# Attention in an encoder block: from 96-row bf16 stacks to paired 64-row fp32r stacks

## What is computed

```python
qkv = layernorm(x) @ qkv_w.T + qkv_b          # 16 heads of 16 channels
q, k = rotary(q), rotary(k)
attn = softmax(einsum('bhqd,bhkd->bhqk', q, k) * D ** -0.5)
x = x + einsum('bhqk,bhkd->bhqd', attn, v).reshape(B, L, C) @ proj_w.T + proj_b
x = x + cross_attention(layernorm(x), ctx)
x = x + experts(layernorm(x))                 # each expert takes its top 512 tokens
```

## Time and profile before

| | |
|---|---|
| median of 3 runs | 1540.33 us (1540.18 to 1541.49) |
| profiled execution | 1540.64 us, span 1538.8 us |
| busy in the span: PE, DVE, ACT, POOL | 84%, 74%, 50%, 23% |
| mean granted TensorE clock | 0.886 of full |

### The profile page before, as it was taken

The page is one execution under the profiler, slowest core; times in us unless marked ns, Lnnn a source line. Parts: engine busy times, 40 slices in busy tenths (PEclk is TensorE's granted clock), DMA queues, the critical chain, the costliest instruction groups (busy, mean ns, idle before and its releaser), DMA issues. The chain is left out here.

```text
span 1538.8 us, 21970 instructions
## 1 busy us (share of the span) xinstructions
PE 1297.3 (84%) x7046; PEld 618.8 (40%) x7046; DVE 1132.2 (74%) x2543; ACT 770.7 (50%) x984; POOL 354.2 (23%) x327
## 2 busy tenths in 40 slices
PE   5777488999999999999999999976788613799995
PEld 3444212222222222222222222235677602678794
DVE  6888487889888898789888898325777487677751
ACT  2333203666666666566666666833434311365652
POOL 3777530000000000000000000011332102266654
PEclk9888656999999999999999999986778655899998
DMA  3246492023330333113331200041232101163532
GB/s 118 93 150 192 155 192 56 20 48 62 60 60 12 59 63 60 30 40 62 60 63 21 47 7 5 9 140 45 95 99 82 55 4 55 43 156 99 158 86 28
DMA packets 100871, 111.19 MB, mean 72 GB/s; under 512 B 24992, under 2 KB 77984, under 8 KB 99744
## 3 DMA queue, kind: packets, MB, share of 16 engines
q1 hardware_dynamic: 94624, 101.50, 25.7%
q0 software_dynamic: 6144, 8.39, 2.9%
HBM read 71.73 MB, written 37.75 MB: 71 GB/s over the span
## 5 line engine op out<-in xcount | busy, mean ns | idle before, releaser
L623 DVE TENSOR_REDUCE b_max_halves<-banks 128x1 f32<-128x512 f32 x1024 | 635.8, 683 | 82.4 <-PE banks L678 70.1
L591 ACT ACTIVATE b_probs<-banks 128x1024 f32<-128x1024 f32 x512 | 496.5, 1021 | 313.9 <-PE banks L736 312.7
L678 PE MATMUL banks<-b_k,b_q 96*128 96x512 bf16 x1024 | 354.7, 401 | 30.8 <-DVE b_identb L644 17.3
L736 PE MATMUL banks<-b_q,b_k 99*128 99x512 bf16 x1024 | 302.1, 382 | 1.7 <-DMA b_q<-b_max_rows 0.2
L703 PE MATMUL banks<-b_probs,b_v 128*32 128x512 f32 x2048 | 274.5, 608 | 0.5 <-ACT b_probs L591 0.5
L678 PEld LDWEIGHTS banks<-b_k,b_q 96*128 96x128 bf16 x1024 | 85.0, 97 | 410.0 <-DVE b_max_halves L623 351.0
L607 POOL TENSOR_SCALAR b_minus_max<-b_max 128x32 f32<-128x32 f32 x16 | 4.6, 290 | 741.4 <-DVE b_max L627 741.4
L736 PEld LDWEIGHTS banks<-b_q,b_k 99*128 99x128 bf16 x1024 | 94.2, 98 | 109.0 <-ACT b_probs L591 55.6
L1373 POOL DMA_INDIRECT e_x<-rows,d_idx x32 | 52.3, 1635 | 127.0 <-DVE d_wx L1554 64.1
L359 PE MATMUL banks<-a_w,a_xnT 128*128 128x512 f32 x128 | 73.4, 703 | 1.2 <-issue 1.2
L1682 PE MATMUL banks<-e_w2h,e_hTh 128*128 128x256 f32 x256 | 73.8, 288 | 0.0
(11 more groups left out here) (228 smaller groups left out, 1710.1 us busy)
## 6 DMA issues: line engine op xcount, KB each, us to landing
e_w<-in_w SPq DMA_DIRECT2D x16, 1024.0 KB, 8.3
v_tiles<-a_v SPq DMA_DIRECT2D x8, 1024.0 KB, 6.0
b_v<-v_tiles SPq DMA_DIRECT2D x16, 512.0 KB, 9.7
q_stacks<-a_parts SPq DMA_DIRECT2D x24, 256.0 KB
k_stacks<-a_parts SPq DMA_DIRECT2D x24, 256.0 KB
b_q<-q_stacks SPq DMA_DIRECT2D x16, 384.0 KB, 4.9
b_k<-k_stacks SPq DMA_DIRECT2D x16, 384.0 KB, 8.0
a_x<-in_x SPq DMA_DIRECT2D x8, 512.0 KB, 4.4
```

The source lines that it names most:

```text
L591: nc.scalar.activation(pr[:, u, s % 2], ps[:, 2 * u:2 * u + 2, :], ACT.Exp, scale=D ** -0.5).then_inc(s_ex[u], 1)
L623: v.tensor_reduce(mxp[:, par].rearrange("p j t h -> p (j t h)")[:, k:k + 1], ps[:, bank(last), :], AX.X, ALU.max).then_inc(s_mr, 1)
L678: nc.tensor.matmul(ps[:, bank(m), :], qs[g][0:RQ, j, P * t:P * t + P], ks[g][0:RQ, j, CH * kh:CH * kh + CH], start=True, stop=True).then_i ...
L736: ins = nc.tensor.matmul(ps[:, j, :], ks[g][0:RQ + 3, j, P * (s % KT):P * (s % KT) + P], qs[g][0:RQ + 3, j, CH * (s // KT):CH * (s // KT) ...
```

## The change

**In project_qkv** q and k are split in two fp32r parts: ACT copies the first and DVE subtracts for the second. The third part, the second copy by ACT and POOL's share are gone. The stacks in DRAM have 32 rows of f32 for a head where they had 48 of bf16. `store_qk` waits for all four `f` and then issues 8 DMAs of 512 KB. The reuse of `a_parts` waits for them as before.

**In attend** a head's stack is 48 rows (three part-products), padded with zeros up to row 62; rows 62 and 63 hold the maximum's two parts in q and -1 in k. Two heads lie in rows 0 to 63 and 64 to 127. Scores and maxima are issued as pairs, one for each half of the rows. A group `g` is now worked as two halves `hg` of 512 queries (32 in all), with maxima, rows and output for each. Every step has 4 maxima; 48 are made ahead of the first step. `values` is issued in two halves of 256 queries. The output isn't transposed: SP takes the sums row of `osb` to `sT` by 4 DMAs (`sums`), DVE takes reciprocals (`invert`, in step 3 of the next `hg`), SP writes them to DRAM and reads them back spread over rows (`spread`, 1 and 4 DMAs), POOL multiplies (`scale`), and SP stores (4 DMAs). The rows of maxima take 8 DMAs. `load_group` has 9. POOL zeroes the padding.

**In cross_attend** `attended` is loaded with channels in rows, and its transposes and copies are gone. In experts one wait takes another constant.

```diff
@@ project_qkv @@
             def store_qk(i):
+                sp.wait_ge(s_pb[1], 4 * i + 4)
                 for f in range(4):
-
-                    sp.wait_ge(s_pc[f % 2], 4 * i + 2 + f // 2 + 1)
-                    for m in range(3):
+                    for m in (1, 0):
...
             def split(i, h, f):
                 if h == 0:
-                    act.wait_ge(s_qs[f], 48 * i)
+                    act.wait_ge(s_qs[f], 32 * i)
                 act.wait_ge(s_rt, 8 * i + 4 * h + f + 1)
                 half = slice(CH * h, CH * h + CH)
                 nc.scalar.activation(parts[:, f, 0, half], ps[:, 6 + f % 2, :], ACT.Copy).then_inc(s_pa, 1)
-                act.wait_ge(s_r, 8 * i + 4 * h + f + 1)
-                nc.scalar.activation(parts[:, f, 1, half], rest[:, f % 2, :], ACT.Copy).then_inc(s_pb, 1)
@@ load_group @@
+    for s in range(2):
+        heads = slice(G * g + s, G * g + G, 2)
+        for dst, src, runs in ((q, qst, ((0, 0, 16), (16, 0, 32))), (k, kst, ((0, 0, 32), (32, 0, 16)))):
+            for to, lo, n in runs:
+                sp.dma_start(dst[HR * s + to:HR * s + to + n, :, :].bitcast(F32),
+                             src[b][heads][:, lo:lo + n, :].rearrange("h r n -> r h n")).then_inc(s_ld, 16)
@@ attend, SP @@
+            sp.wait_ge(s_minus, 1)
+            ones(0)
             for g in range(1, 3):
+                sp.wait_ge(s_clear[g], 4)
                 load(0, g)
+            sp.wait_ge(s_ra, 1)
+            rows(0, 0)
...
+                    if h == 0:
+                        if not (first and g == 0):
+                            sp.wait_ge(s_pv, 8 * (8 * i + hg))
+                        if not (last and g > 0):
+                            if g == 0:
+                                if first:
+                                    sp.wait_ge(s_clear[3], 4)
+                                load(i, 3)
+                            else:
+                                load(i + 1, g - 1)
+                    back = not (first and hg == 0)
+                    m, x = 8 * i + hg - 1, (hg - 1) % 2
+                    if back:
+                        sums(m, x)
+                        spread(m, x)
+                    if not (last and hg == NH - 1):
+                        sp.wait_ge(s_ra, n["rows"] + hg + 1)
+                        rows((hg + 1) // 2 % NG, (hg + 1) % 2)
+                    if back:
...
@@ attend, DVE @@
+            def invert(n, x):
+                dve.wait_ge(s_sum, 16 * G * n + 16 * G)
+                v.reciprocal(rT[:, x, :], sT[:, x, :]).then_inc(s_rec, 1)
...
+                            if place == 1 and kt == 3 and not (first and hg == 0):
+                                invert(8 * i + hg - 1, (hg - 1) % 2)
@@ attend, PE @@
+                stack = slice(HR * s, HR * s + RS)
+                at = CH * h + P * t
+                nc.tensor.matmul(ps[:, bank(last), :], qs[g][stack, p, at:at + P],
+                                 ks[g][stack, p, CH * kh:CH * kh + CH], start=True, stop=True).then_inc(s_mm, 1)
...
+                        for u in range(2):
+                            pe.wait_ge(s_ex[u], 64 * i + S)
+                            scores(g, h, S, u, 0)
+                            scores(g, h, S, u, 1).then_inc(s_st[u], 1)
+                            for x in range(2):
+                                ring(hg, kt, u, x)
+                            if u == 0:
+                                earlier(S, 2, 1)
+                            else:
+                                earlier(S, 1, 0)
```

More of the change, by code:

```diff
@@ L336, in body @@
                         rotate(i, h, t)
-                        if t % 2 == 0 and not (first and h == 0):
-                            split(*away(i, h, -1), t)
             bodies(pool, body)
-            for f in range(0, 4, 2):
-                split(B - 1, 1, f)
         @block.tensor
@@ new lines, in attend, with count, before @@
+        START = [("max", k) for k in range(NB)] + [("rows", 0)] + [("max", k) for k in range(NB, AHEAD)]
+        def count(items, kind):
+            return sum(k == kind for k, _ in items)
+        def before(i, first):
+            if first:
+                return {"items": len(START), "max": AHEAD, "rows": 1}
+            return {"items": (MAXS + NH) * i + len(START), "max": MAXS * i + AHEAD, "rows": NH * i + 1}
+        assert len(plan(False)[1]) == MAXS + NH and (MAXS + NH) % NR == 0 and len(START) % NR == 1
@@ new lines, in body @@
+            def body(i, first, last):
+                for hg in range(NH):
+                    for kt in range(KT):
+                        S = KT * hg + kt
+                        if kt == 1 and not (first and hg == 0):
+                            take(8 * i + hg - 1, (hg - 1) % 2)
+                        for u in range(2):
+                            act.wait_ge(s_st[u], 64 * i + S + 1)
+                            if not first or S >= NP:
+                                act.wait_ge(s_pv, 64 * i + S - NP + 1)
+                            nc.scalar.activation(pr[:, S % NP, u], ps[:, 2 * u:2 * u + 2, :], ACT.Exp,
@@ new lines, in values @@
+            def values(i, S, half):
+                hg, kt = S // KT, S % KT
+                if half == 0:
+                    if kt == 0:
+                        pe.wait_ge(s_oe, 8 * i + hg)
+                    for u in range(2):
+                        pe.wait_ge(s_ex[u], 64 * i + S + 1)
+                elif kt == 0:
+                    return
+                at = slice(0, CH) if kt == 0 else slice(HC * half, HC * half + HC)
+                for j in range(G):
+                    last = nc.tensor.matmul(ps[VW * j:VW * j + VW, PV, at], vs[hg // 2][:, kt, j, :],
+                                            pr[:, S % NP, j // 2, j % 2, at], start=(kt == 0),
+                                            stop=(kt == KT - 1 and half == 1))
+                if half or kt == 0:
+                    last.then_inc(s_pv, 1)
@@ L714, in body, with ring @@
+            pe.wait_ge(s_ld[0], LD)
+            pe.wait_ge(s_zero, 1)
+            none = {"max": 0, "rows": 0}
+            for m, (kind, k) in enumerate(START):
+                if kind == "max":
+                    maxima(k, none, START, m, m)
+                else:
+                    rows(k, none, START, m, m)
+            pe.wait_ge(s_one[0], 32)
             def body(i, first, last):
-                at = plan(first, last)[0]
-                def ring(g, s, place):
-                    for kind, k, m in at[g, s, place]:
+                at, items = plan(last)
+                n = before(i, first)
+                def ring(hg, kt, place, x):
+                    for kind, k, m in at[hg, kt, place][x:x + 1]:
@@ L719, in ring @@
                         if kind == "max":
-                            maxima((g + 1) % NG, k, base(i, first), m)
-                        elif kind == "out":
-                            outputs(2 * (4 * i + g) - k, base(i, first), m)
-                        else:
-                            rows(4 * i + g + 1, base(i, first), m)
-                for g in range(NG):
-                    n = 4 * i + g
-                    pe.wait_ge(s_row[g], 16 * i + 16)
-                    if not (last and g == NG - 1):
+                            maxima(k, n, items, m, len(START) + m)
+                        else:
+                            rows(8 * i + k, n, items, m, len(START) + m)
@@ new lines, in scores, with earlier @@
+                def scores(g, h, S, u, s):
+                    kt = S % KT
+                    stack = slice(HR * s, HR * s + HR)
+                    return nc.tensor.matmul(ps[:, 2 * u + s, :], ks[g][stack, u, P * kt:P * kt + P],
+                                            qs[g][stack, u, CH * h:CH * h + CH], start=True, stop=True)
+                def earlier(S, back, half):
+                    if S >= back:
+                        values(i, S - back, half)
+                    elif not first:
+                        values(i - 1, KT * NH + S - back, half)
@@ L730, in body @@
+                for hg in range(NH):
+                    g, h = hg // 2, hg % 2
+                    pe.wait_ge(s_row[h], 512 * i + 128 * g + 128)
+                    if first and h == 0 and g < NG - 1:
+                        pe.wait_ge(s_one[g + 1], 32)
+                    if h == 0 and not (last and g == NG - 1):
                         pe.wait_ge(s_ld[(g + 1) % NG], LD * i + (2 * LD if g == NG - 1 else LD))
-                    for s in range(STEPS):
+                    for kt in range(KT):
+                        S = KT * hg + kt
```

472 lines of the change are left out of this document (219 added, 253 removed).

## The result

The changed kernel took 1587.57 us (median of 4 runs), against 1540.61 us for the kernel before (median of 4 runs): a ratio of 1.029, 95% interval 1.025 to 1.033. The forecast was 1510 us, so the sign was wrong. The time lies above the forecast's own range (1465 to 1555) and just inside the wide one (1420 to 1590). The profiled execution took 1588.24 us, with a span of 1586.4 us and a mean granted clock of 0.843, where the kernel before had 0.886.

The account below looks back on a forecast made before the run. PE was taken to set attend's 3.15 us step, with DVE close behind. 1540.6 + 0 (project_qkv) - 16 (start) - 16 (steps) + 12 (end) - 11 (cross_attend) = 1510 us; own range 1465 to 1555, 8 in 10: 1420 to 1590.

Parts of the forecast that it names:

- rival 2: In attend's steps, a third weight load can't start under a matmul in its own rows: say 1557 us; chance 0.20.
- project_qkv, 0: First stage: DVE's dropped third parts against larger stores that begin later, net 0 us (from -15 to +8).
- 6.7 us in each of three batches, 20 back: In project_qkv, time lost again as ACT waits for the stores of all four `f` to land.
- Attend's start, -16: Before the first step: 48 reduces instead of 64, 48.4 us to 32.1; gain 10 if rows' DMAs don't fit.
- The stops, 90 us: In attend's steps, DVE's reciprocal waits for sums queued behind the group's load: 12 x 7.5 us.
- The `hg`, 20.4 us: In attend, eight steps of 2.50 us with PE and DVE near each other: 20.4 us allowed for each `hg`.
- The chain of small DMAs, 13 us: In attend's steps without a load, rows land after PE wants them, 0 to 2 us each: 19 x 0.7.
- the loop's turn: In attend's steps, a stop where the loop turns, 5 us, as the stop near 636 us.
- Attend's end, +12: After the last step: copy, sums, reciprocal, DRAM and back, POOL and store take 16.5 us, before 4.7.
- cross_attend, -11: Stage behind attend: no transposes and copies, 3.2 us off the first half, 1.1 for each of seven others.
- Rival 1: In attend's steps, the sums aren't held behind the load, so the 90 us go: 1420 us; chance 0.14.
- Rival 3: In attend's steps, pairs of 64-row matmuls run singly, half steps of 1.58 us: 1635 us; chance 0.13.

Follow-up runs that it names:

- the kernels above: The follow-up kernels, each the changed kernel with edits to DMA order, queue, waits, maxima or matmul order; 1437.7 to 1632.8 us.
- the single waits: Each of the four stores of q and k in project_qkv waits for its own parts alone, against the changed kernel: 1550.0 us.

## Why the prediction was wrong

The forecast said 31 us less, it became 48 more in the profiled execution. That the time still lies in the wide range is luck: the range reached to 1590 for rival 2, whose mechanism did not come about. The 79 us between them, by the steps of the prediction:

- **project_qkv, 0: measured +14.7.** The step that failed is "6.7 us in each of three batches, 20 back". I saw that the stores begin behind all four `f` and costed the wait as a transfer of 5.1 us for each `f` at 205 GB/s, the fourth landing at 22.5. In the trace the first store is issued at 114.7, and ScalarE could write `f` = 0 again at 124.5, 1 at 129.7, 2 at 134.6 and 3 only at 142.5: the first landing takes 10 us, not 7, and the last comes 28 behind, not 22.5.

```profile
114.69 5.96 SPq L158 DMA_DIRECT2D q_stacks<-a_parts  x4
```

```profile
142.49 0.60 ACT L212 ACTIVATE a_parts<-banks 128x512 fp32r<-128x512 f32 x1 [7.27 <-DMA k_stacks<-a_parts]
```

The next loads of x and the stores of v share the queue, which no run here took apart. The last batch's compute ends at 197.5, where I had 177.4; attend begins 13.3 us behind that, where I had 19. Taking the one wait apart again gave 28.9 us.
- **Attend's start, -16: measured -7.** I wrote that the rows' DMAs fit beside the last maxima "though they stand behind two loads". They didn't: 10.6 us. My alternative, a gain of 10, was nearer. That a second and a third cause stood behind this one I had not seen.
- **The stops, 90 us: about 114.** Right in kind, place and number (L681, behind the load, 12 within the steps). A stop is 9.5 us, not 7.5: 6.8 idle instead of 6.0, and 2.7 of low clock instead of 1.5, since the clock came back only after three half steps where I had taken the 4 us behind a shorter stop. That is +24.
- **The `hg`, 20.4 us: 21.3.** The half step came as forecast (1.25 to 1.27), but "With two engines that near each other I allow 20.4" allowed too little: DVE alone is at 1.22, PE alone at 1.23, and neither can give way to what the other has besides. 30.5 x 0.9 is +28.
- **The chain of small DMAs, 13 us: about 7** of waits for rows by PE, beside 5 for the loop's turn as forecast. `hg`, last steps, stops, rows and turn make 650 + 24 + 114 + 7 + 5 = 800 of the 806 us.
- **Attend's end, +12: +9.4**, in the order foretold.
- **cross_attend, -11: -5** for all stages behind attend. The same code there took between 512 and 524 us from the last reciprocal to the end in the kernels above (524 in the change), so a term of this size can't be told from one profile; it also means that the 6 us that the single waits gained behind attend are not shown to be theirs.

Rival 1, the sums not held, is out: they are. Rival 2 is out by its price: half a step is 1.25 to 1.27 us, under the 1.36 from which it would decide. In the trace the third weight load starts 0.11 us behind the first pair, under matmuls of 0.50 us in the same rows. The Trainium skill ("TensorE: Matmul & The Clock Gate", part 3, what overlaps and what doesn't) states that LDWEIGHTS overlaps matmuls in flight only where the row group differs, and by that rule it would wait for the first of them; this trace disagrees, with the 0.11 us. Rival 3, pairs run singly, is out as well. The loss came not from any rival of mine but from terms of the forecast itself: three waits that I had named and taken too small (the stores', the first rows', the sums') and the pace of the half step. What erred the other way, the chain by 6 us and attend's end by 3, was small. The arithmetic saved is sure only where an engine stays busy, and the waits set against it came from a few rows each.

## What to carry to other kernels

When a kernel's order of DMAs in one queue changes, write down for each small transfer what was issued ahead of it, and for each wait of the issuing engine what is queued behind it: spread thin in another queue the load cost at most 0.9 us, but with 2 KB transfers behind it, it cost a group of two `hg` 9.5 us, and moving those ahead brought back 4.6 and handed the rest to the next ones (the rows; in another order the reciprocals, and at the start the -1 rows). The best that was tried for a large background transfer is another queue and small doses over the whole stretch, the two together. A stop costs its idle time and the half clock behind it, here 2.7 us on top of 6.8; and a wait pulled out of a loop (all four instead of each) can cost more than the arithmetic that was saved.

## What the chip did that I had not expected

- Two 64-row matmuls ran at the same time whatever stood between them in the program: two weight loads of 191 ns in 0.19 us, and both scores started ahead of the first maxima in either order. A half step with four such matmuls took 1.23 us where PE alone set it.
- A second queue isolates only partly: the sums took 7.3 us to land behind the load in one queue, 4.0 in a queue beside it, 2.3 beside a load spread thin (medians over all `hg` between 300 and 640 us).
- Eight rows' DMAs of 2 KB take 5.03 us to issue on SP, 0.63 each. The second `hg`'s eight took 8.72 behind a load.
- The order of three groups of DMAs on one engine moved this kernel between 1523.8 and 1632.8 us with the same work.
